# Two graph attention layers on one core: layer 1 one chunk further behind layer 0, and features made in two mixed slots a batch

## What is computed

```python
h = jnp.maximum(_layernorm(x, axis=-1), 0.0)
f = jnp.einsum('bnf,of->bno', h, W)                     # (layer 1: + b, per head)
e = leaky_relu((f @ a_src)[:, :, None] + (f @ a_dst)[:, None, :], 0.2)
e = jnp.where(adj == 0, NEG_INF, e)
x = x + jnp.einsum('bij,bjo->bio', softmax(e, axis=-1), f)
```

## Time and profile before

| | us |
|---|---|
| median of 3 runs | 2947.19 (2942.62 to 2951.24) |
| profiled execution as a whole | 2948.32 |
| its span, first to last instruction | 2946.5 |
| PE busy | 2518.9 (85%) |
| DVE busy | 2008.4 (68%) |
| ACT busy | 1624.0 (55%) |
| POOL busy | 1359.3 (46%) |
| mean granted clock of PE | 0.94 |

### The profile page before, as it was taken

The page is one execution under the profiler, slowest core; times in us unless marked ns, Lnnn a source line. Parts: engine busy times, 40 slices in busy tenths (PEclk is TensorE's granted clock), DMA queues, the critical chain, the costliest instruction groups (busy, mean ns, idle before and its releaser), DMA issues. The chain is left out here.

```text
span 2946.5 us, 61722 instructions
## 1 busy us (share of the span) xinstructions
PE 2518.9 (85%) x22166; PEld 2262.9 (77%) x22166; DVE 2008.4 (68%) x3326; ACT 1624.0 (55%) x3058; POOL 1359.3 (46%) x1757
## 2 busy tenths in 40 slices
PE   5987999879998799978999699997999979996686
PEld 4876888768887688867888488885888858885586
DVE  1558766587666676676666667757676587675896
ACT  4026655565555655556555565565555566563564
POOL 2113544435554444453554535553444535444566
PEclk9998999989999899998999899998999989998899
DMA  7731333223332133322333223332244213301010
GB/s 129 75 49 30 62 63 55 37 37 61 61 51 52 25 63 64 47 49 33 61 61 45 51 34 61 61 57 43 38 73 63 46 30 54 54 16 23 16 39 18
DMA packets 197681, 146.23 MB, mean 50 GB/s; under 512 B 143072, under 2 KB 144224, under 8 KB 197472
## 3 DMA queue, kind: packets, MB, share of 16 engines
q1 hardware_dynamic: 179040, 110.07, 15.4%
q0 software_dynamic: 18432, 33.56, 13.9%
HBM read 193.60 MB, written 50.66 MB: 83 GB/s over the span
## 5 line engine op out<-in xcount | busy, mean ns | idle before, releaser
L670 ACT ACTIVATE shared<-Rb,w 128x512 int8<-128x512 f32 x1728 | 1076.8, 718 | 388.0 <-DVE shared L1113 387.7
L842 PE MATMUL accA<-S,shared 128*128 128x257 f32 x4096 | 976.0, 391 | 87.6 <-DVE shared L1048 83.4
L861 PE MATMUL accB<-Sw,shared 128*128 128x195 bf16 x7680 | 977.4, 250 | 81.6 <-DVE shared L1117 80.7
L842 PEld LDWEIGHTS accA<-S,shared 128*128 128x128 f32 x4096 | 772.6, 194 | 197.7 <-DVE shared L1048 96.0
L867 PE MATMUL accB<-Sv,shared 128*128 128x130 f16 x7680 | 763.8, 223 | 0.0
L861 PEld LDWEIGHTS accB<-Sw,shared 128*128 128x128 fp8e4 x7680 | 640.8, 98 | 132.9 <-issue 94.2
L1048 DVE SCALAR_TENSOR_TENSOR shared<-Rb,w,mask 128x512 f32<-128x512 f32 x512 | 427.7, 849 | 404.4 <-PE accA L842 355.7
L867 PEld LDWEIGHTS accB<-Sv,shared 128*128 128x128 fp8e4 x7680 | 577.7, 99 | 0.8
L489 POOL TENSOR_SCALAR shared<-shared 128x260 f32<-128x260 f32 x128 | 124.8, 975 | 759.6 <-ACT shared L712 754.2
L1113 DVE TENSOR_TENSOR shared<-shared,mask 128x512 uint32<-128x512 uint32 x432 | 325.6, 754 | 190.9 <-ACT shared L670 152.1
L1117 DVE TENSOR_TENSOR shared<-shared,mask 128x512 uint32<-128x512 uint32 x512 | 392.7, 767 | 8.9
(11 more groups left out here) (103 smaller groups left out, 2370.9 us busy)
## 6 DMA issues: line engine op xcount, KB each, us to landing
Rb<-R_dram SPq DMA_DIRECT2D x160, 256.0 KB, 3.4
adj_bytes<-in_adj POOLq DMA_DIRECT2D x128, 256.0 KB, 5.3
xb<-in_x SPq DMA_DIRECT2D x32, 512.0 KB, 3.8
out<-xb SPq DMA_DIRECT2D x32, 512.0 KB, 2.8
mask<-adj_bytes SPq DMA_TRANSPOSE x128, 4.4
shared<-in_W SPq DMA_DIRECT2D x2, 256.0 KB, 2.9
R_dram<-R_rows SPq DMA_DIRECT2D x8, 32.0 KB, 1.8
a_cols<-in_a SPq DMA_DIRECT2D x8, 0.2 KB, 10.5
```

The source lines that it names most:

```text
L670: last = nc.scalar.activation(cmp[:, slot, jj // 2, of_pair(jj % 2, 0, CI)], Rb[:, h, :], ACT.Sign, bias=w[1][:, JG * g + jj, h:h + 1], sc ...
L842: last = nc.tensor.matmul(accA[:, k, 0:F + 1], tiles[:, j % RING, k * P:(k + 1) * P], S0[:, j, 0:F + 1], start=j == 0, stop=j == NJ - 1)
L861: nc.tensor.matmul(acc[:, bank, col:col + NS], bits[:, g % BRING, 1, jj // 2, of_pair(jj % 2, k * P, P)], Sw[:, j, h, :, :].rearrange("p a ...
```

## The change

Layer 1 trails layer 0 by five chunks in place of four (B_LAG = NC + 1). In the batch b >= 1 the chunk 0 of layer 0 has no layer 1 chunk beside it, and the last chunk of layer 1 of the batch before has no layer 0 chunk beside it. These two places become mixed slots: **slot F** holds the chunk 0 of layer 0 of batch b and the making of layer 1's features of batch b - 1; then come three combined steps (layer 0's chunk c beside layer 1's chunk c - 1); **slot G** holds the last layer 1 chunk of batch b - 1 and the making of layer 0's features of batch b + 1. The features stage is gone, but for three: layer 0 of batch 0, layer 0 of batch 1, and layer 1 of the last batch are made alone. In the last batch G has no features beside it.

```diff
-    XSLOTS = 2 * NC
-    MSLOTS = NC + 2
+    XSLOTS = 2 * NC + 1
+    MSLOTS = NC + 3
+    B_LAG = NC + 1
...
+        def batch(prog, b, more):
+            prog.slot_f(b)
+            for c in range(1, NC):
+                prog.step("AB", (STEP_AB if more else STEP_AB_LAST)[c], b, c)
+            if more:
+                prog.slot_g(b)
+            else:
+                prog.step("G", STEP_B, b, NC)
+        def start(prog):
+            prog.features(0, 0)
+            prog.first_chunk()
+            for c in range(NC):
+                prog.step("A", STEP_A[c], 0, c)
+            prog.step("A", STEP_A_END, 0, NC - 1)
+            prog.features(1, 0)
+        def end(prog):
+            batch(prog, B - 1, False)
+            prog.features(B - 1, 1)
+            for c in range(1, NC + 1):
+                prog.step("B", STEP_B, B, c)
...
+        def looped(eng, prog):
+            start(prog)
+            with eng.Fori(1, B - 1) as b:
+                batch(prog, b, True)
+            end(prog)
```

PE, ACT and DVE use `looped`, with no inner loop; POOL and SP are written out. The order of PE in the two slots (T transposes, FE projections, MX, MN, RW the turn of the maxima, the mean and the turn of the rows):

```diff
+            def slot_f(b):
+                events = [("T", 0), ("FE", 0), ("T", 1), ("A", 0), ("FE", 1), ("T", 2), ("A", 1), ("FE", 2), ("T", 3),
+                          ("A", 2), ("FE", 3), ("A", 3), ("A", 4), ("MX",), ("A", 5), ("A", 6), ("MN",), ("A", 7),
+                          ("A", 8), ("RW",)] + [("A", j) for j in range(9, NJ)]
+            def slot_g(b):
+                events = [("G", 0, 0), ("G", 0, 1), ("T", 0), ("G", 0, 2), ("G", 0, 3), ("FE", 0), ("T", 1)]
+                events += [("G", 1, i) for i in range(G)] + [("FE", 1), ("T", 2), ("G", 2, 0), ("G", 2, 1), ("FE", 2)]
+                events += [("T", 3), ("G", 2, 2), ("G", 2, 3), ("FE", 3), ("G", 3, 0), ("MX",), ("G", 3, 1), ("MN",)]
+                events += [("G", 3, 2), ("G", 3, 3), ("RW",)]
```

DVE in slot F (MV moves features, W weighs, LF and LS subtract the first and the second part), and ACT in slot G (NY normalises, YT and SF move, EX exponentials, SC scales, Y1 normalises for the next F):

```diff
+                events = [("MV", 0), ("A", 0), ("A", 1), ("MV", 1), ("A", 2), ("A", 3), ("MV", 2), ("A", 4), ("MV", 3),
+                          ("MAX",), ("A", 5), ("SHIFT",), ("W", 0), ("A", 6), ("MEANL",), ("A", 7)]
+                for t in range(NC):
+                    events += [("W", t)] * (t > 0) + [("LF", t), ("A", 8 + 2 * t), ("LS", t), ("A", 9 + 2 * t)]
...
+                events = [("NY", 0), ("G", 0, 0), ("G", 0, 1), ("YT", 0), ("NY", 1), ("G", 0, 2), ("G", 0, 3), ("EB", 0),
+                          ("SF", 0), ("YT", 1), ("NY", 2), ("G", 1, 0), ("G", 1, 1), ("G", 1, 2), ("G", 1, 3), ("EB", 1),
+                          ("SF", 1), ("YT", 2), ("NY", 3), ("G", 2, 0), ("G", 2, 1), ("SF", 2), ("YT", 3),
+                          ("G", 2, 2), ("G", 2, 3), ("EB", 2), ("SF", 3), ("G", 3, 0), ("G", 3, 1), ("EX",), ("SC",),
+                          ("G", 3, 2), ("G", 3, 3), ("Y1",), ("ROWS",), ("EB", 3)]
```

ACT in slot F: it moves the transposed features, normalises and scales layer 0's features (chunks 1 to 3) for each chunk, then the exponentials and the parts. Both casts of Sw and the first of Sv are ACT's now:

```diff
+            def parts(b):
+                first_part(b, 0)
+                move_rows(b, 1)
+                second_part(b, 0)
+                high(b, 0)
+                for t in range(1, NC):
+                    first_part(b, t)
+                    second_part(b, t)
+                    high(b, t)
+                    low(b, t - 1)
+                low(b, NC - 1)
```

More of the change, by code:

```diff
@@ L2 @@
 from concourse import mybir
+from collections import namedtuple
 from contextlib import ExitStack
@@ L299, in gat_two_layers, with written_out @@
+        def written_out(prog):
+            start(prog)
+            for b in range(1, B - 1):
+                batch(prog, b, True)
+            end(prog)
+        def looped(eng, prog):
+            start(prog)
+            with eng.Fori(1, B - 1) as b:
+                batch(prog, b, True)
+            end(prog)
+        Program = namedtuple("Program", "features first_chunk step slot_f slot_g")
         block = ctx.enter_context(nc.Block())
@@ L387, in _ @@
+            written_out(Program(features, lambda: turn_mask(1), step, slot_f, slot_g))
         @block.gpsimd
@@ L871, in steps @@
                         last.then_inc(S["bits_free"], 1)
-            phases(pe, features, steps)
+            looped(pe, Program(features, lambda: None, step, slot_f, slot_g))
         @block.vector
@@ new lines, in features @@
+            def features(b, L):
+                if L == 0:
+                    if b == 0:
+                        for t in range(NC):
+                            statistics0(0, t)
+                else:
+                    for t in range(NC):
+                        move_features(b, t)
+                maxima(b, L)
+                shifted(b, L)
+                if L == 1:
+                    weigh(b, 0)
+                mean(b, L)
+                if L == 1:
+                    for t in range(NC):
+                        if t:
+                            weigh(b, t)
+                        less_first(b, t)
+                        less_second(b, t)
```

875 lines of the change are left out of this document (444 added, 431 removed).

## The result

The changed kernel takes 3018.36 us (median; 3012.87 to 3019.22), the kernel before 2946.53 beside it: ratio 1.0239, 95% interval 1.022 to 1.0259. The change makes the kernel 2.4% slower. The forecast was 3032.

A forecast was written before the change was run, and what follows sets the result against it. Combined steps are bound by PE, features stages by a chain through PE, ACT, DVE and POOL. 190.4 + 7x82 + 25 + 7x212.3 + 6x68 + 148 + 183.7 + 15.8 = 3031, giving 3032 us; range 2925 to 3115.

The forecast's parts named there:

- Slot F: Layer 1 features beside a layer 0 chunk: a chain through engine orders takes 82 us, bounds 73 and 88.
- the 2.4 us for the low clock: Slot F: five tiles, mean and turn at PE's low clock lie on the chain, up to 5 us, 2.4 taken.
- The period: Slot F, from one weighing W of the parts to the next: 9.2 us, as measured before; bounds 7.2 and 9.9.
- The sentence on free tiles (8.5): Slot F: if POOL does not hold DVE's tiles, W's period would be 8.5 us and the sum 3016.
- The 9.3: Slot F: by the skill's rule POOL holds DVE's tiles too, giving W's period 9.3 us and sum 3033.
- Combined steps: Three steps remain per batch: 209.8 us plus 2.5 for the early X1, 212.3 together.
- the 2.5 us for the early X1: First combined step: a second X1 on DVE leaves PE idle 2.5 us; bounds 0, if rings cover it, and 7.
- Slot G: Layer 1 chunk beside layer 0 features: 56.4 us PE work, start and ACT waits make 68; bounds 63 and 74.
- Ends and jump: Batch 1 features 33, plain chunk 49, layer 1 features 66, together 148 us; loop jump 5 us in five of seven F.
- Rival 1: Slot F's parts flow without waiting for rows or mean: F 73, G 64, total 2927 us; chance 0.22.
- Rival 2: Slots F and G save only what they cost, extra pieces at the ends cost: total 2969 us; chance 0.13.
- Rival 3: PE stays at low clock from F's second half, ACT late in G: F 88, G 74, steps 217, total 3142; chance 0.17.

The follow-up runs named there:

- Experiments 1 and 2: Changed kernel with ACT's move of rows behind the second cast, 2993.22 us; then also slot F's mean and turns reordered on PE and DVE, 2964.45 us.
- Experiment 5: Changed kernel with POOL's adjacency load of the first combined step issued behind EB of head 0 instead of ahead of it: 2996.8 us.
- experiment 4: Changed kernel with POOL's subtraction made on one column only and ACT's low cast unscaled: 2963.34 us, one run.
- experiment 9: Changed kernel with ten instead of six comparison groups of slot G on DVE: 2983.82 us; on top of earlier projections in slot G, 2994.32 us.
- experiment 6: Changed kernel with the loop over batches 1 to 6 written out on PE, ACT and DVE: 2986.46 us.
- experiment 3: On top of Experiments 1 and 2: slot F's last nine tiles beside parts chunks 0 to 2, ACT's layer 0 sums behind the last second part: 2930.05 us.
- experiment 1: Changed kernel with ACT's move of the turned rows in slot F put behind the second cast of chunk 0: 2993.22 us.

## Why the prediction was right

**The total: right in direction for its reason, close in part by luck.** 3031 stands against 3016.8 because two errors cancel, 37 us too much in the combined steps and 29.5 too little in slot G. The direction does not hang on them: with the measured steps and G as forecast the sum is 2994, still 1.6% slower.

**Slot F: right, and for its reason.** Take 4.4 us for the jump off the times of batch 2, by which its F is longer than the last (85.68 less 81.30). W0 then starts at 33.0 (said 33.1), the turn of rows ends at 43.0 (43.7), the second cast starts at 43.3 (44.0), tile 9 ends at 46.3 (47.2) and tile 15 at 74.6 (74.8); PE's gap ahead of tile 6 is 2.65 (3). Experiments 1 and 2 took the two waits of this chain away and F fell as it said. Behind tile 15 two terms were off and cancelled: the 2.4 us for the low clock did not appear on the chain (tiles 7 and 8 took PE 3.81 together, the high level), and the rows' load took 5.6 instead of 3.4, beside a load that POOL issues at once, which the forecast had passed over as two steps ahead of need. Experiment 5 shows it. That these two cancel is luck as well.

**The period: right in the choice, a bit long.** 8.76 against 9.2. The sentence on free tiles (8.5) leaned on rows 8, where no tile was held so long; with POOL's 3.17 us pieces they are. The forecast took the measured period of the old stage, which had such holds in it. Of the Trainium skill's rule it is the mechanism that agrees (experiment 4). The 9.3 that the forecast worked out by it was 0.5 too long: not each tile of a chunk meets POOL's subtraction, one does (2.66) and the other does not (0.74).

**Combined steps: mis-sized, 37 us too much.** The step that failed is the 2.5 us for the early X1, and that the first step starts like the others. In the first step PE idles 1.0 us in all (67.65 less 66.61), and that at its end, ahead of the next step's first tile; in the next two it idles 4.1 and 3.0, together 8.2 against 3 x 4.9 + 2.5 = 17.2. PE's busy time is 198.7 against the 3 x 65.2 = 195.6 that go with that sum, which takes back 3 of these 9 us. The rings cover the early X1 whole, which was the lower bound; and the first step has no X1 at the end of the slot ahead of it, since F has none. The kernel before shows what that is worth: of its four steps the one behind the features stage, which has no X1 either, has 1.5 us of idle PE where the next has 4.9:

```profile
265.44:334.65 69.21, 67.71 (x641) 62.35 (x641) 46.57 (x81) 43.06 (x77) 25.40 (x36) 0.96 0.23 34
```

**Slot G: mis-sized, 29.5 us too little.** Every wait was as forecast: the start 3.70 + 1.53 = 5.2 (5.3), the first projections 3.48 (3.4), the second 1.24 (1.5), the fourth 1.42 (1.4). What failed is the 56.4 us of PE work, taken at the high clock: it was 61.47 at a granted clock of 0.91 (and 57.8 at 0.97 in experiment 9, so about 1 us of it is not the clock). Behind the wait of 3.48 us FE ran at 3.81 for 1.96, at the lower of the two levels, as did the matmuls of the first groups behind the wait of 3.70 at the start (0.86 for 0.50, from 888.6 to 895.3). Behind the waits of 1.24 and 1.42 it stayed at the high one (2.01). The rate after idle time stood in the forecast for a tile (3.3 against 1.8) and was used in F, not here. The lower bound of 63 is not its own sum either: 56.4 and the start of 5.3 are 61.7.

**Ends and jump.** The features of layer 1 alone took 63.5 instead of 66: either the casts on ACT give more than 4, or EB and the normalisation cost less than 3; no run tells these apart. The jump, put at 5 us in five slots, 25 in all, is 4.6 in five; with 1.2 less in the first F and 0.2 in the last, the seven F give 24.5 (experiment 6).

**Rivals.** Rival 1 (F 73, G 64) did not come: the second part started behind the turned rows. Experiments 1 and 2 made its condition true, and F came near it, 75.2 where there is no jump, but G stayed at 71.6 and the time at 2964. The kernel of experiment 3 comes to its total, 2930 where the rival said 2927, but by another sum, and that is chance: its seven F are 71.0 in the mean with the jumps (the rival 76.6), its G 71.5 (64). Rival 2's mechanism, the pieces at the ends, is 15 of the 70 us; the F and G of a batch did not save what they cost but took 158.5 us with the jump, where a stage and a step took 147.6. Rival 3's F 88 and steps of 217 did not come, its G of 74 nearly did.

## What to carry to other kernels

Two stages laid beside each other share not only engines but orders: each instruction that one chain needs soon must not stand behind a tile, a move or a comparison of the other, and the queue of every engine is to be walked for it. A few lines of order (experiments 1 to 3) decided here between 2.4% slower and 0.7% faster. When a slot's engine waits, cost the work behind the wait at the lower clock too, and look at what the late engine does in that slot before changing its order: in slot G the new order only moved the wait, and taking work off the engine gained 6.2 us.

## What was not expected of the hardware

- Behind a wait of 3.48 us TensorE ran the next pieces at half rate (3.81 us for 1.96, 1.91 for 1.04); behind 1.03 us of idle time at the same place it ran them at the full rate (2.01, 1.03).
- A 256 KB load from SyncE's queue landed in 3.0 us alone and in 5.6 beside a 256 KB load of POOL's queue issued in the same microsecond.
- The jump of the loop costs 4.6 us a turn in slot F, while PE's own gap is 2.57, and 5.9 in the features stage of the kernel before, where the gap is 4.7 to 5.3. Writing the loop out saved 32 us in the changed kernel and 45 in the kernel before; 24.5 and 30 are found in these slots and stages, the rest is open.
- Slot G with the same instructions and nearly the same idle time of PE (11.2 and 11.5 us) took 70.4 or 73.0 us at a granted clock of 0.95 or 0.91 (experiment 1). Slot F of one kernel took 83.3 at 0.88 or 85.6 at 0.80, with 5.3 us more of busy PE (experiment 5). What decides the clock is open.
